# A gated feed-forward product by Strassen's seven block products instead of eight, with its second product summed in SBUF

## The reference

```
mod = (silu(c) @ wmod).reshape(2, 6, 1, 512)        # shift, scale and gate, twice
h = layernorm(x) * (1 + ca) + sa
x = x + ga * (h @ masked(weight).T + bias)           # "attention": one product
h = layernorm(x) * (1 + cb) + sb
h1 = lora(h, w1); h3 = lora(h, w3)                   # 512 -> 1376, with rank-16 additions
x = x + gb * lora(silu(h1) * h3, w2)                 # 1376 -> 512
```

## Time and profile before

| | us |
|---|---|
| median of 3 runs (264.52 to 265.27) | 264.66 |
| the profiled execution's own time | 267.26 |
| its span, first to last instruction | 265.7 |
| TensorE busy in it | 248.6 |
| VectorE, ScalarE, GpSimd busy | 125.5, 86.5, 61.7 |

### The profile page before, as it was taken

The page is one execution under the profiler, slowest core; times in us unless marked ns, Lnnn a source line. Parts: engine busy times, 40 slices in busy tenths (PEclk is TensorE's granted clock), DMA queues, the critical chain, the costliest instruction groups (busy, mean ns, idle before and its releaser), DMA issues.

```text
span 265.7 us, 3341 instructions
## 1 busy us (share of the span) xinstructions
PE 248.6 (94%) x1205; PEld 197.6 (74%) x1205; DVE 125.5 (47%) x208; ACT 86.5 (33%) x144; POOL 61.7 (23%) x75
## 2 busy tenths in 40 slices
PE   7799975989989999999999999999999999999990
PEld 6577773668768888888888877888888888888770
DVE  3516864669979985475465542351222112220144
ACT  2326776063624346545633320111111011110100
POOL 1326789512632313123201000060000000000012
PEclk9979998999999999999999999999999999999997
DMA  6999930006122341322324600037000000000004
GB/s 186 388 381 417 407 129 1 5 2 215 58 100 79 121 118 41 121 79 63 95 81 122 34 3 2 0 16 156 28 0 0 1 2 0 0 0 2 0 0 158
DMA packets 12371, 23.99 MB, mean 90 GB/s; under 512 B 1218, under 2 KB 2498, under 8 KB 12356
## 3 DMA queue, kind: packets, MB, share of 16 engines
q1 hardware_dynamic: 12208, 23.65, 28.9%
q10 hardware_dynamic: 148, 0.14, 0.2%
HBM read 21.16 MB, written 2.10 MB: 88 GB/s over the span
## 4 chain that ended last, share of the span: by engine, by line
PE 79%; DVE 6%; ACT 5%; issue 4%; DMA 2%; POOL 2%; SPq 0%; DVEq 0%; ACTq 0%; POOLq 0%
PE up_a L1050 21%; PE up_b L1050 21%; PE acc L1064 8%; PE acc L1065 8%; PE acc L1063 8%; PE acc L1001 4%; DMA xt<-in_x 2%; PE side L1031 2%; ACT ht_hi L513 1%; DVE stats L652 1%; PE acc L907 1%; ACT work L496 1%; PE side L919 1%; PE side L1035 1%; DVE parts L732 1%
## 5 line engine op out<-in xcount | busy, mean ns | idle before, releaser
L846 DVE TENSOR_TENSOR g<-up_b,g 128x512 f32<-128x512 f32 (+1 forms) x22 | 15.2, 690 | 73.2 <-PE up_b L1050 73.2
L1064 PE MATMUL acc<-w_lo,g_hi 128*128 128x512 f32 (+1 forms) x88 | 34.7, 394 | 0.0
L1065 PE MATMUL acc<-w_hi,g_lo 128*128 128x512 f32 (+1 forms) x88 | 34.7, 394 | 0.0
L1063 PE MATMUL acc<-w_hi,g_hi 128*128 128x512 f32 (+1 forms) x88 | 34.6, 394 | 0.0
L408 POOL TENSOR_TENSOR xt<-work,xt 128x512 f32<-128x512 f32 x5 | 6.8, 1382 | 112.7 <-DVE work L771 112.7
L756 DVE SCALAR_TENSOR_TENSOR raw<-side,raw 128x512 f32<-128x512 f32 (+2 forms) x33 | 21.4, 676 | 24.0 <-PE side L1031 17.4
L622 ACT ACTIVATE g<-up_a 128x512 f32<-128x512 f32 (+1 forms) x22 | 13.1, 597 | 59.5 <-PE up_a L1050 59.5
L627 ACT ACTIVATE g_hi<-g 128x512 fp32r<-128x512 f32 (+1 forms) x22 | 13.9, 632 | 52.9 <-DVE g L846 52.9
L544 ACT ACTIVATE w_hi<-raw 128x512 fp32r<-128x512 f32 (+2 forms) x33 | 20.1, 625 | 22.9 <-DVE raw L756 22.9
L1050 PE MATMUL up_a<-ht_hi,w_hi 128*128 128x512 f32 (+1 forms) x88 | 24.4, 398 | 0.4 <-ACT w_hi L544 0.4
L1050 PE MATMUL up_a<-ht_hi,w_lo 128*128 128x512 f32 (+1 forms) x88 | 24.1, 395 | 0.0
(11 more groups left out here) (151 smaller groups left out, 352.1 us busy)
## 6 DMA issues: line engine op xcount, KB each, us to landing
raw<-in_ffn SPq DMA_DIRECT2D x33, 256.0 KB, 2.6
wmod_sb<-in_wmod SPq DMA_DIRECT2D x4, 1024.0 KB, 11.1
xt<-in_x SPq DMA_DIRECT2D x8, 256.0 KB, 8.4
wmod_sb<-in_wmod SPq DMA_DIRECT2D x1, 2048.0 KB, 15.4
out<-xt SPq DMA_DIRECT2D x8, 256.0 KB, 2.9
mask_sb<-in_mask SPq DMA_DIRECT2D x4, 256.0 KB, 10.5
wa<-in_weight SPq DMA_DIRECT2D x4, 256.0 KB, 10.6
lora_raw<-in_lora SPq DMA_DIRECT2D x2, 320.0 KB, 8.2
```

The lines of the kernel that those rows point to most:

```text
L846: nc.vector.tensor_tensor(g[0:w], up_b[0:w], g[0:w], ALU.mult).then_inc(g_ready, 1)
L1063: nc.tensor.matmul(acc[t][:], hi, down_hi[j][0:w], start=(j == 0), stop=False)
L1064: nc.tensor.matmul(acc[t][:], hi, down_lo[j][0:w], start=False, stop=False)
L1065: last = nc.tensor.matmul(acc[t][:], lo, down_hi[j][0:w], start=False, stop=(j == HT - 1))
```

## The change

The products up of ten 128-row hidden tiles are made in five pairs. In a pair the weights are a 2 x 2 grid of blocks (two tiles x two halves of the features), and so are the tokens (two halves of the features x two batches). Strassen's scheme makes the four block results from seven block products in place of eight, by sums of blocks: of weights T1 to T4 (`weight_sums` and `weight_sums_after` on GpSimd), of tokens S1 to S4 (`token_sums`, `token_sum_4` on VectorE, `token_sum_3` on GpSimd), and of products (`add_u2`, `add_u3`, `add_c22`, `add_c21`, `add_c12` on VectorE, `p1_copy` on ScalarE). Each product is made twice, for w1 (u = 2i) and for w3 (u = 2i + 1). The 96-row tile comes first, by `up0`, once for each batch. Since the token sums need both batches, batch 1's second norm moves ahead of the first pair.

The products down are made per pair and token group (`down(i, place)`, six matmuls into one of three banks) and added into SBUF by `down_add`; those of the 96-row tile (`down(-1, n)`, three matmuls) are copied there by `down0_copy`. The groups of pair i - 1 stand between the block products of pair i. GpSimd makes three of the four g of a pair (`g_mult`) and all their low parts (`g_low`). In the last pair GpSimd multiplies the sums by the gate and adds x ahead of the last groups (`out_prepare`), and `down_end` and `add_x2` add these. The slots in `raw` are 8 instead of 4. The weight tiles live in ten slots for blocks and four for the products down.

The diff, cut to the orders on the engines and the functions that matter for them:

```diff
-SLOTS = 4
+SLOTS = 8
+BLOCKS = 7
+BLOCK_SLOTS = 10
+DOWN_SLOTS = 4
...
-X1_POOL = (0, 1, 2, 4, 5, 6, 7)
-X2_POOL = (0, 1, 2, T, T + 2)
...
+WHOLE_DVE = (9, 11, 12, 13, 14, 15)
+X1_POOL = (0, 1, 2, 4, 5)
+LAST_ORDER = (4, 5, 6, 7, 0, 1, 2, 3)
+X2_POOL = (4, 5, 6, 0, 1)
...
+        def group_bank(g):
+            return acc[1 + g % 3]
...
+            def weight_sums(i):
...
+                nc.gpsimd.tensor_tensor(tsum[:, 0], b12, b11, ALU.subtract).then_inc(sums_ready, 1)
+                pool.wait_ge(merged, stream_of(i, 3) + 1)
+                pool.wait_ge(sums_ready, 4 * i + 1)
+                nc.gpsimd.tensor_tensor(tsum[:, 1], b22, tsum[:, 0], ALU.subtract).then_inc(sums_ready, 1)
+            def weight_sums_after(i):
...
+                nc.gpsimd.tensor_tensor(b12, b22, b12, ALU.subtract).then_inc(sums_ready, 1)
+                pool.wait_ge(sums_ready, 4 * i + 2)
+                pool.wait_ge(w_ready, item_of(i, B21) + 1)
+                nc.gpsimd.tensor_tensor(b21, b21, tsum[:, 1], ALU.subtract).then_inc(sums_ready, 1)
+            def token_sum_3():
+                pool.wait_ge(s1_ready, KT // 2)
+                for c in range(KT // 2):
+                    nc.gpsimd.tensor_tensor(h1[:, c], h0[:, c], h1[:, c], ALU.subtract).then_inc(s3_ready, 1)
...
+            def g_mult(i, n):
+                signal, src = ((c22_ready, u3), (c21_ready, p1), (c12_ready, u2))[n]
+                pool.wait_ge(signal, 2 * i + 2)
+                pool.wait_ge(silu_ready, 4 * i + 2 + n)
+                nc.gpsimd.tensor_tensor(cbuf[:, 1 + n], src[:, 1], cbuf[:, 1 + n], ALU.mult).then_inc(g_by_pool, 1)
+            def g_low(i, n):
+                b, e = ((0, 0), (1, 1), (1, 0), (0, 1))[n]
+                pool.wait_ge(g_high_ready, 4 * i + n + 1)
+                nc.gpsimd.tensor_tensor(g_lo[b][e][:], cbuf[:, n], f32(g_hi[b][e][:]), ALU.subtract).then_inc(g_low_ready, 1)
+            def out_prepare(n):
+                b, t = divmod(n, T)
+                pool.wait_ge(down_added, group_of(PAIRS - 2, n) - TILES + 1)
+                pool.wait_ge(gate_row_loaded[b], 16 * KT)
+                nc.gpsimd.tensor_tensor(out_sum(n), out_sum(n), gate_row[:, b], ALU.mult).then_inc(out_scaled, 1)
+                pool.wait_ge(out_scaled, n + 1)
+                nc.gpsimd.tensor_tensor(out_sum(n), out_sum(n), xt[:, b, t], ALU.add).then_inc(out_ready, 1)
...
+                pool.wait_ge(down_gated, LAST_ORDER.index(n) + 1)
+                pool.wait_ge(out_ready, n + 1)
+                nc.gpsimd.tensor_tensor(xt[:, b, t], raw[:, n], out_sum(n), ALU.add).then_inc(x2_by_pool, 1)
...
             spread(1)
             spread(2)
+            add_x1(4)
+            add_x1(5)
             root(3 * T, 2)
             root(3 * T + 2, 2)
+            low(12)
+            low(13)
+            g0_low(0)
+            weight_sums(0)
+            token_sum_3()
+            weight_sums_after(0)
+            spread(3)
             spread(4)
+            token_low(S3)
+            token_low(S4)
+            g0_low(1)
+            for i in range(PAIRS):
+                if i + 1 < PAIRS:
+                    weight_sums(i + 1)
+                    weight_sums_after(i + 1)
+                else:
+                    for n in range(T):
+                        out_prepare(n)
+                if i + 2 < PAIRS:
+                    spread(2 * i + 5)
+                    spread(2 * i + 6)
+                g_low(i, 0)
+                g_mult(i, 0)
+                g_low(i, 1)
+                g_mult(i, 1)
+                g_low(i, 2)
+                g_mult(i, 2)
+                g_low(i, 3)
+            for n in range(T, TILES):
+                out_prepare(n)
+            for n in LAST_ORDER:
...
+            def p1_copy(u):
+                i, second = divmod(u, 2)
+                act.wait_ge(p1_out, u + 1)
...
+                nc.scalar.activation(p1[:, second], up_a[:], ACT.Copy).then_inc(p1_ready, 1)
...
+            def g_high(i, n):
+                b, e = ((0, 0), (1, 1), (1, 0), (0, 1))[n]
+                if n == 0:
+                    act.wait_ge(g11_ready, i + 1)
+                else:
+                    act.wait_ge(g_by_pool, 3 * i + n)
...
+                nc.scalar.activation(g_hi[b][e][:], cbuf[:, n], ACT.Copy).then_inc(g_high_ready, 1)
...
+            weight_high(item_of(0, B11))
             for n in range(LORA_EARLY, len(LORA_CUTS)):
                 lora_high(n)
+            silu0(0)
+            weight_high(item_of(0, B21))
+            norm(3 * T)
+            norm(3 * T + 1)
+            p1_copy(0)
+            g0_high(0)
+            silu(0, 0)
+            high(12)
+            high(13)
+            high(14)
+            high(15)
+            p1_copy(1)
+            weight_high(item_of(0, T1))
+            weight_high(item_of(0, T2))
+            for n in range(T):
+                down0_copy(n)
+            silu0(1)
+            weight_high(item_of(0, T3))
+            weight_high(item_of(0, T4))
+            weight_high(item_of(0, B22))
+            token_high(S2)
+            token_high(S1)
+            token_high(S3)
+            token_high(S4)
+            g0_high(1)
+            for i in range(PAIRS):
+                more = i + 1 < PAIRS
+                if i:
+                    p1_copy(2 * i)
...
+                silu(i, 1)
...
+                if i:
+                    p1_copy(2 * i + 1)
+                if more:
+                    weight_high(item_of(i + 1, T2))
+                g_high(i, 0)
+                if more:
+                    weight_high(item_of(i + 1, T3))
+                g_high(i, 1)
+                if more:
+                    weight_high(item_of(i + 1, T4))
+                g_high(i, 2)
+                if more:
+                    weight_high(item_of(i + 1, B22))
+                g_high(i, 3)
...
+            def add_u3(u):
+                dve.wait_ge(p7_out, u + 1)
...
+                nc.vector.tensor_tensor(u3[:, second], up_b[:], p1[:, second], ALU.add).then_inc(u3_ready, 1)
+            def add_c22(u):
+                dve.wait_ge(p5_out, u + 1)
+                dve.wait_ge(u3_ready, u + 1)
+                nc.vector.tensor_tensor(u3[:, u % 2], acc[0][:], u3[:, u % 2], ALU.add).then_inc(c22_ready, 1)
...
+            def down_end(place):
+                n = LAST_ORDER[place]
                 b, t = divmod(n, T)
+                g = group_of(PAIRS - 1, place)
+                dve.wait_ge(down_out, g + 1)
                 dve.wait_ge(gate_row_loaded[b], 16 * KT)
+                nc.vector.tensor_tensor(raw[:, n], group_bank(g)[:], gate_row[:, b], ALU.mult).then_inc(down_gated, 1)
                 if n in X2_POOL:
                     return
+                dve.wait_ge(down_gated, place + 1)
+                dve.wait_ge(out_ready, n + 1)
+                nc.vector.tensor_tensor(xt[:, b, t], raw[:, n], out_sum(n), ALU.add).then_inc(x2_by_dve, 1)
...
+            merge(3)
+            attn_gate(4)
+            attn_gate(5)
+            weight_low(2)
+            weight_low(item_of(0, B11))
+            attn_gate(6)
+            attn_gate(7)
+            add_x1(6)
+            add_x1(7)
+            moment(12)
+            moment(13)
+            merge(4)
+            moment(14)
+            moment(15)
+            weight_low(item_of(0, B21))
+            centres(12)
+            g0(0)
+            norm(14)
+            norm(15)
+            whole(12)
+            whole(13)
+            whole(14)
+            whole(15)
+            low(14)
+            low(15)
+            g11(0)
+            merge(5)
+            merge(6)
+            token_sums()
+            lora_part(3)
+            lora_part(4)
+            merge(7)
+            merge(8)
+            weight_low(item_of(0, T1))
+            weight_low(item_of(0, T2))
+            token_sum_4()
+            weight_low(item_of(0, T3))
+            weight_low(item_of(0, T4))
+            weight_low(item_of(0, B22))
+            token_low(S2)
+            token_low(S1)
+            add_u2(0)
+            g0(1)
+            for i in range(PAIRS):
+                more = i + 1 < PAIRS
+                r = stream_of(i + 1, 0)
+                u = 2 * i
+                if i:
+                    add_u2(u)
+                if more:
+                    merge(r)
+                    merge(r + 1)
+                weight_low(item_of(i, BLOCKS))
+                weight_low(item_of(i, BLOCKS + 1))
+                if more:
+                    merge(r + 2)
+                add_u3(u)
+                add_c22(u)
+                if more:
+                    merge(r + 3)
+                if i:
+                    down_add(i - 1, 0)
+                    down_add(i - 1, 1)
+                if more:
+                    merge(r + 4)
+                add_c21(u)
+                if more:
+                    weight_low(item_of(i + 1, B11))
+                add_c12(u)
+                if more:
+                    weight_low(item_of(i + 1, B21))
```

(131 more changed lines are left out.)

624 lines of the change are left out of this document (369 added, 255 removed).

## The result

The changed kernel takes 325.38 us (median of 4 runs, 323.6 to 326.27) beside 264.75 for the kernel before on the same chip (4 runs, 264.52 to 265.27): 1.228 times as long (95% interval 1.222 to 1.234). I had forecast 298 us, 282 to 308. The direction was right; of 60.6 us I had 33.3.

The account below looks back on a forecast made before the run. TensorE's matmuls were taken to bound the kernel before. Dense work 251.7 plus idle 24.0 (front), 6.9 (pair 0), 7.5 (pairs 1 to 3) and 8.9 (tail) gave span 299.0, median 298 us, range 282 to 308.

Parts of the forecast that it names:

- Dense work: Whole span if TensorE stayed dense: sixty fewer matmuls, 14.0 us less, giving 251.7 us.
- Front: From attend_last to down(-1, 4): in-order queues outlast TensorE's 27.0 us of work, leaving it 24.0 us idle (19.4 to 27.3).
- the sign: Said to show the forecast right: TensorE idle 4 us or more ahead of the fourth narrow group down.
- the middle of 109.4 to 117.3: End of g0_low(1) before down(-1, 4): 109.4 without VectorE-GpSimd meetings, 117.3 if they always exclude each other; 114 taken.
- Pair 0: From down(-1, 4) to down(0, 0): 26.5 us where matmuls and merges are 19.6, so 6.9 idle (5.4 to 7.9).
- Pairs 1 to 3: Ahead of each pair's down(i, 0): GpSimd's g chain takes 12.5 us against TensorE's 10.0, 2.5 a pair, 7.5 for three.
- The clock rival: At each pair boundary the clock falls too, four times 1.5 us: 304, or 310 with high ends; chance 0.10.
- Tail: From down(3, 0) to the span's end: 54.5 us through GpSimd's queue, 8.85 more than dense matmuls and the earlier tail.
- TensorE stays the bound: Whole kernel: the other engines have room, so span 251.7, median 250.6, faster than before; chance 0.07.
- The meetings seldom happen: VectorE and GpSimd seldom hinder each other, so all terms take their low ends: 286 us; chance 0.15.

Follow-up runs that it names:

- all mends: The changed kernel with second buffers for g_high(i, 1), g_mult and out_prepare on VectorE, and the front's queues reordered: 285.56 us, 1.075 times the kernel before.

## Why the prediction was right in direction and wrong in size

The 325.38 us lie above the range of 282 to 308. The step that failed is the way to down(i, 0) in pairs 1 to 3 and in the last pair: it held a wait for a buffer that the sum put at nothing. The half clock behind the waits is the second part, which the sum left to a rival of 0.10.

**Dense work, 251.7**: right. The sixty matmuls went, and no load is late: no stop of TensorE behind attend_last ended on a DMA.

**Front, 24.0 us idle**: right. attend_last started at 60.76, 27.0 us of work would end at 87.8, down(-1, 4) started at 112.33: 24.6, of which TensorE stood for 18.7; the rest is for the most part half clock, which the sum held for p2 and the first transposes alone. The idle ahead of p2_product is 4.89 on ScalarE's p (said 4.9), down(-1, 3) waits until 92.79 for ScalarE's copies of the narrow groups (said 93.8), a wait of 3.54 where the sign asked for 4; the clock there is 0.77. The four spreads that I priced at 2.4 us took 6.08, so the choice above the middle of 109.4 to 117.3 held. (The prediction has a front in which the two engines always exclude each other 2 us longer than 114; by its own sum it is 3.3, 117.3 less 114.)

**Pair 0, 26.5 us**: 30.0. The matmuls behind down(-1, 4) ran at half clock until about 119, some 2.7 us that the sum did not hold; the idle times themselves came to 7.1 (6.07, 0.79, 0.27), beside 6.9.

**Pairs 1 to 3, 2.5 us each: the step that failed.** Ahead of down(1, 0) TensorE waited for 6.58 us. I summed "add_u3 and add_c22 (1.55) and three turns (9.9)" and 1.0 for meetings, 12.5, and let the first turn start as soon as c22 was there. In the profile the way from the end of p7 (166.0) to down(1, 0) is 16.5: 1.6 for the sums, three turns of 3.7, and 3.74 for a wait that I had not followed. The code of g_high names it: the single buffer, read until the last group of the pair before. I followed each wait of GpSimd's list and, on ScalarE, only the one for GpSimd's product. With a second buffer TensorE's wait is 2.9 us, where I had 2.5: the rest of the sum stood, the turns of 3.7 us for 3.3 being about the 1.0 for meetings.

**The clock rival, 0.10**: wrong in weight. I set it aside because 2.5 us are shorter than the 3.16 of the earlier trace rows. At 6.6 us there was no doubt left: in the changed kernel every down(i, 0) starts at half clock, and a pair of 40.2 us is 32.2 of matmuls, 6.58 of wait and 1.4 lost to the clock. Filling the waits gave back 8.4 us. The comparison with 3.16 would not have held at the forecast's own waits either: in the run with the second buffer, behind 2.90 us ahead of down(2, 0), the clock was 0.94 over pair 3, and with the products on VectorE, behind 2.72 us ahead of down(0, 0), it was 0.54 for the first 3.1 us. The Trainium skill (TensorE: Matmul & The Clock Gate, Part 1) has the half rate as what TensorE falls back to without activity; the run with the filled waits agrees, with 1.00 for 0.92 in pairs 1 and 2.

**Tail, 54.5**: 60.9, and all of it ahead of down(4, 0), which comes 35.5 us after down(3, 0) where I had 29.45: the same buffer (GpSimd stands for 4.86 us there) and the same clock. From down(4, 0) to the end it is 25.4, and I had 25.05, with GpSimd's queue busy almost without a break from 294.75 to 319.96 and the last group alone behind 4.60 us of wait.

**TensorE stays the bound, 0.07**: it stood for 22% of the span. **The meetings seldom happen, 0.15**: they happened; g_mult averages 1.62 us, not 1.27, and 1.26 where VectorE stood still in the last pair.

By cause: the missed wait is 3.74 us in one pair, 4.86 - 0.74 = 4.1 in the last, so some 15 in four (taking it away gave 13.3 of span, a little of it by the clock), and the clock 8.4 by the run that filled the waits ahead of down(i, 0). No run has both mends, and a shorter wait may cost less clock, so that they add is not shown; if they do, they are some 22 of the 25.7 us that were missing.

## What to carry to other kernels

When a value passes through several engines, follow every semaphore of every hop, the ones that guard the buffer it is written to as much as those that bring its inputs: a single buffer that the next stage reads to its end turns two stages into a line. Price a TensorE wait together with the half clock that may follow it, by rows of waits of like length and not by a single one, and see whether harmless work can fill it. An operation moved from a busy engine to an idle one can be paid again in part where VectorE and GpSimd then meet: count both queues' two-operand work in the same stretch, and keep GpSimd's instructions short where VectorE is the one in a hurry.

## What was not expected of the hardware

A VectorE subtract with two SBUF operands took 6.32 us, nine times its usual 0.68, beside back-to-back GpSimd instructions, and two of GpSimd's 128-wide spreads took 8.24 us, where they take 1.17 to 1.3; the first of them, 6.96 us, lay beside eight VectorE operations with two SBUF operands, one right behind the other. The Trainium skill (SBUF — State Buffer, section Who interferes with whom) has the engine that issues first hold the shared port for a whole instruction; the run with the halved lows agrees, as the longest low fell from 6.32 to 1.77 us, but that one operation is passed over for three instructions of the other engine in turn, and another for eight, is more than the rule says.

Equal waits did not cost equal time. Behind a wait of 6.07 us the changed kernel had a clock of 0.58 from 142.4 to 146.0 and 1.00 from there, and pair 1 took 40.2 us; with the narrowed sums, behind a wait of 6.11, the clock was 0.50 from 138.9 to 143.0 and still 0.80 to 147.0, and pair 1 took 41.3. Nor does the wait's length alone tell whether the clock falls. In the run with the second buffer the waits ahead of down(1, 0) and down(2, 0) are both 2.90 us; behind the first the clock stays at 1.00 over the whole pair, behind the second it falls:

```profile
181.40:216.50 35.10, 32.20 (x142) 26.18 (x143) 22.98 (x35) 10.91 (x20) 18.09 (x15) 1.00 0.18 47
216.50:253.20 36.70, 33.55 (x141) 27.08 (x141) 23.04 (x35) 10.97 (x20) 15.35 (x11) 0.94 0.22 14
```

The fall can also come when TensorE is at work again: with all mends, behind 2.72 us ahead of down(0, 0), the first matmul took 0.47 us, and yet the clock was 0.60 from 133.7 to 138.0. So the first matmul alone does not tell. What decides it these runs do not show, and about 1 us a pair hangs on it.
